# Lookup scores from stacked one-pass operands, aggregates scaled on ScalarE: one change after the attention of a fused block

## What is computed

```python
x = x + _layernorm(attention(_layernorm(x)))      # 16 heads of 16
h = _layernorm(x)
query = h @ q_proj_w.T                            # 128 wide
rq = query @ router_w.T                           # 48 wide
rk = aux_keys @ router_w.T                        # 1024 keys, 48 wide
scores = rq @ rk.T / sqrt(48) + reliability_mask
top_scores, top_idx = top_k(scores, 8)
w = softmax(top_scores)
agg = einsum('bsk,bskh->bsh', w, aux_values[top_idx])
# gate: sigmoid of the row's log variance over its mean, and of a small gelu network on h
out = h + gate[..., None] * agg
x = x + _layernorm(out)
```

## Time and profile before

| | |
|---|---|
| median of 3 runs | 3106.18 us (3104.97 to 3108.98) |
| the profiled execution | 3108.23 us, its span 3106.4 us |
| TensorE busy | 3056.3 us (98%) |
| VectorE busy | 2822.5 us (91%) |
| ScalarE busy | 2489.8 us (80%) |
| GpSimd busy | 244.1 us (8%) |
| granted TensorE clock, mean | 0.985 of 2.4 GHz |
| lookup stage, from the first `lookup_scores` | 2819 to 3106 us of the span |

### The profile page before, as it was taken

How to read it: one execution, slowest core, us unless ns; L and a number is a source line. 1 busy time by engine, 2 the same in 40 slices (tenths; PEclk the granted TensorE clock), 3 DMA queues, 4 the chain that set the end, 5 groups by cost and what they waited for, 6 DMA issues and landing times.

```text
span 3106.4 us, 67882 instructions
## 1 busy us (share of the span) xinstructions
PE 3056.3 (98%) x26937; PEld 1337.5 (43%) x26937; DVE 2822.5 (91%) x3050; ACT 2489.8 (80%) x4539; POOL 244.1 (8%) x798
## 2 busy tenths in 40 slices
PE   8999999999999999999999999999999999999997
PEld 4544443443444343444444344344444344345765
DVE  5599999999999999999999999999999999957776
ACT  6278888888888888888888888888888888864444
POOL 2400000000000000000000000000000000001012
PEclk9799999999999999999999999999999999999999
DMA  7420101010110101010202010101001010000001
GB/s 261 63 42 1 39 5 35 8 29 15 22 22 15 28 11 33 5 39 1 42 1 42 1 39 5 32 12 25 18 18 25 15 28 16 16 1 1 1 8 48
DMA packets 27400, 83.03 MB, mean 27 GB/s; under 512 B 4657, under 2 KB 15649, under 8 KB 24034
## 3 DMA queue, kind: packets, MB, share of 16 engines
q1 hardware_dynamic: 26834, 77.84, 10.8%
q0 software_dynamic: 272, 1.05, 0.1%
HBM read 57.90 MB, written 20.97 MB: 25 GB/s over the span
## 4 chain that ended last, share of the span: by engine, by line
PE 92%; DVE 4%; ACT 2%; issue 1%; DMA 0%; POOL 0%; ACTq 0%; DVEq 0%; POOLq 0%
PE ps L1152 43%; PE ps L1161 37%; PE ps L1128 3%; PE ps L1087 2%; PE ps L1171 1%; PE ps L1349 1%; PE ps L1101 1%; PE ps L1179 1%; PE ps L1079 1%; PE ps L1294 1%; DVE partial L790 1%; DVE k_raw L861 1%; DVE q_raw L854 1%; ACT k_raw L633 1%; DVE q_raw L851 1%
## 5 line engine op out<-in xcount | busy, mean ns | idle before, releaser
L790 DVE TENSOR_REDUCE partial<-ps 128x1 f32<-128x1024 f32 x2048 | 2485.9, 1224 | 130.6 <-PE ps L1128 116.2
L568 ACT ACTIVATE work<-ps 128x512 f32<-128x512 f32 x4096 | 2207.7, 597 | 361.5 <-PE ps L1152 163.7
L1128 PE MATMUL ps<-k_stack,q_stack 48*128 48x512 f32 x4096 | 1533.1, 453 | 5.5 <-DVE partial L790 5.5
L1152 PE MATMUL ps<-q_stack,k_stack 64*128 64x512 f32 x4096 | 1510.1, 448 | 0.3 <-ACT work L568 0.3
L1161 PE MATMUL ps<-work,v_head 128*32 128x256 f32 x16384 | 1296.5, 391 | 0.0
L1152 PEld LDWEIGHTS ps<-q_stack,k_stack 64*128 64x128 f32 x4096 | 632.0, 184 | 805.5 <-ACT work L568 672.1
L1128 PEld LDWEIGHTS ps<-k_stack,q_stack 48*128 48x128 f32 x4096 | 634.3, 187 | 45.9 <-DVE partial L790 40.6
L1161 PEld LDWEIGHTS ps<-work,v_head 128*32 128x32 f32 x16384 | 329.2, 108 | 698.8 <-ACT work L568 579.5
L421 POOL CAST nm_parts<-negmax 128x4 bf16<-128x4 f32 x128 | 24.8, 194 | 2275.7 <-DVE negmax L797 2275.7
L1349 PE MATMUL ps<-k_raw,q_raw 128*128 128x256 f32 x512 | 123.1, 396 | 8.3 <-DVE attn L871 8.3
L560 ACT ACTIVATE q_stack<-ps 3x512 fp32r<-3x512 f32 x128 | 75.1, 587 | 52.5 <-PE ps L1179 49.5
(11 more groups left out here) (127 smaller groups left out, 1000.5 us busy)
## 6 DMA issues: line engine op xcount, KB each, us to landing
k_stack<-qk_parts SPq DMA_DIRECT2D x96, 256.0 KB, 4.1
q_stack<-qk_parts SPq DMA_DIRECT2D x96, 256.0 KB, 4.1
qk_parts<-qk_part SPq DMA_DIRECT2D x32, 512.0 KB, 2.8
x_sb<-L_attn_x SPq DMA_DIRECT2D x8, 512.0 KB, 11.0
out<-k_raw SPq DMA_DIRECT2D x4, 512.0 KB, 3.0
out<-v_head SPq DMA_DIRECT2D x3, 512.0 KB, 2.9
k_raw<-L_ffn_aux_values SPq DMA_DIRECT2D x1, 1024.0 KB
work<-L_attn_w_qkv POOLq DMA_DIRECT2D x1, 768.0 KB, 7.5
```

What stands on the lines that cost most here:

```text
L568: act.activation(probs[:, g % DEPTH, a, :], ps[:, bank, :], ACT.Exp, scale=SCALE).then_inc(exp_done, 1)
L790: dve.tensor_reduce(partial[:, k // 4, k % 4:k % 4 + 1], ps[:, 2 * slot:2 * slot + 2, :], AX.XY, ALU.max).then_inc(max_used, 1)
L1128: last = pe.matmul(ps[:, 2 * slot + e, :], q_stack[HALF:HALF + ROWS, b1, c * CH + (k // 4) * P:c * CH + (k // 4 + 1) * P], k_stack[HALF:HA ...
L1152: pe.matmul(ps[:, bank, :], k_stack[0:HALF, b, P * g:P * (g + 1)], q_stack[0:HALF, b, at:at + CH], start=True, stop=True).then_inc(s_ready, 1)
```

## The change

- The scores are made from fp32r operands, which are rounded and go through TensorE in one pass. `ru` has the rounded rq in rows 0 to 63 and, new, what rounding left in rows 64 to 127. `rk_parts` has the rounded keys twice, one copy under the other, and their rest likewise. Two matmuls per bank give the sum of all four products. The rest of rq is made by a new VectorE step, `route_low`, once per chunk; the keys are split once, by four VectorE steps during the last attention pass.
- `gelu` reads PSUM itself, with the bias, as `ru`'s upper half is taken.
- The scaled copy of the aggregate (`keep_agg`) moves from VectorE to ScalarE, in front of each `move_wT`.
- In chunks 4 to 6 `norm_transpose` of the next chunk moves behind `aggregate(n - 1)`, and `lookup_scores(n + 3)` ahead of `transpose_picked(n + 1)`.

```diff
+        rk_parts = nc.alloc_sbuf_tensor_at("rk_parts", [P, 2, N], F32R, offset=q_at + 4 * T)
+        ru = sb("ru", [P, CH], F32R)
-        ru = work[:, 6144:6656]
...
-                act.activation(ru, ps[:, 3, :], ACT.Identity, bias=rbias).then_inc(r_ready, 1)
+                act.activation(ru[0:RUS, :], ps[0:RUS, 3, :], ACT.Identity, bias=rbias[0:RUS, :]).then_inc(r_ready, 1)
...
-                act.wait_ge(r_ready, c + 1)
-                act.activation(g1T[RUS:RUS + F1, :], ru[RUS:RUS + F1, :], ACT.Gelu).then_inc(u_ready, 1)
+                act.wait_ge(r_psum, c + 1)
+                act.activation(g1T[RUS:RUS + F1, :], ps[RUS:RUS + F1, 3, :], ACT.Gelu, bias=rbias[RUS:RUS + F1, :]
+                               ).then_inc(u_ready, 1)
...
+            def keep_agg(n):
+
+                act.wait_ge(agg_psum, n + 1)
+                act.wait_ge(wr_ready, n + 1)
+                act.activation(attn_rows[:, n, :], ps[:, 2, 0:C], ACT.Copy, scale=wrec[:, n % TPC:n % TPC + 1]
+                               ).then_inc(agg_ready, 1)
+
+            def tile_copies(n):
+
+                if n >= 2:
+                    keep_agg(n - 2)
+                move_wT(n)
...
-            move_wT(n + 3)
+            tile_copies(n + 3)
+            keep_agg(NT - 2)
             normalise(7)
+            keep_agg(NT - 1)
             normalise(8)
...
+                if n >= TPC:
+                    dve.wait_ge(agg_ready, n - TPC + 1)
                 dve.wait_ge(e_ready, n + 1)
...
-            def keep_agg(n):
-
-                dve.wait_ge(agg_psum, n + 1)
-                dve.wait_ge(wr_ready, n + 1)
-                dve.tensor_scalar(attn_rows[:, n, :], ps[:, 2, 0:C], wrec[:, n % TPC:n % TPC + 1], None,
-                                  ALU.mult).then_inc(agg_ready, 1)
+            def route_low(c):
+
+                dve.wait_ge(r_ready, c + 1)
+                dve.scalar_tensor_tensor(out=ru[RUS:P, :], in0=ps[0:RUS, 3, :], scalar=rbias[0:RUS, :],
+                                         in1=ru[0:RUS, :].bitcast(F32), op0=ALU.add, op1=ALU.subtract).then_inc(low_ready, 1)
...
+            dve.wait_ge(w3_e, 4)
+            for at in (0, RUS):
+                dve.tensor_copy(rk_parts[at:at + RUS, 0, :], rkT[0:RUS, :]).then_inc(rk_own, 1)
+            dve.wait_ge(rk_own, 2)
+            for at in (0, RUS):
+                dve.tensor_tensor(rk_parts[at:at + RUS, 1, :], rkT[0:RUS, :], rk_parts[0:RUS, 0, :].bitcast(F32),
+                                  ALU.subtract).then_inc(rk_own, 1)
             dve.tensor_copy(wcat[:, :, 0:RD], ps[:, 2, 2 * P:3 * P].rearrange("p (k n) -> p k n", k=CC)[:, :, 0:RD]
...
                 projected_stats(ahead)
+                route_low(c + 1)
                 take_top(n + 3)
...
-                pe.wait_ge(r_ready, n // TPC + 1)
+                pe.wait_ge(low_ready, n // TPC + 1)
+                if n == 0:
+                    pe.wait_ge(rk_own, 4)
...
                 for a in range(2):
-                    last = pe.matmul(sc_banks(n)[:, a, :], ru[0:RUS, P * i:P * (i + 1)],
-                                     rkT[0:RUS, CH * a:CH * (a + 1)], start=True, stop=True)
+                    for part in range(2):
+                        last = pe.matmul(sc_banks(n)[:, a, :], ru[:, P * i:P * (i + 1)],
+                                         rk_parts[:, part, CH * a:CH * (a + 1)], start=(part == 0), stop=(part == 1))
...
-                if c + 1 < NC:
                     norm_transpose(c + 1, wT_ready, n + 1)
                 if c > 0:
                     aggregate(n - 1)
+                if NC <= ahead and c + 1 < NC:
+                    norm_transpose(c + 1, wT_ready, n + 1)
+                    lookup_scores(n + 3)
...
-                lookup_scores(n + 3)
+                if ahead < NC or c + 1 == NC:
+                    lookup_scores(n + 3)
```

More of the change, by code:

```diff
@@ L234, in sandwich_kernel @@
         w3_e = sem("w3_e")
+        rk_own = sem("rk_own")
         pow_own = sem("pow_own")
@@ L247, in sandwich_kernel @@
         r_ready = sem("r_ready")
+        low_ready = sem("low_ready")
         u_ready = sem("u_ready")
@@ L667, in _ @@
                 n = c * TPC
-                move_wT(n)
+                tile_copies(n)
                 move_hT(c + 1)
@@ L673, in _ @@
                 exponentials(n + 2)
-                move_wT(n + 1)
+                tile_copies(n + 1)
                 move_ru(c + 1)
@@ L683, in _ @@
                 exponentials(n + 3)
-                move_wT(n + 2)
+                tile_copies(n + 2)
                 if c == 5:
@@ L972, in _ @@
             block_stats(3)
+            route_low(0)
             take_top(0)
@@ L980, in tile_turn @@
             def tile_turn(n):
-                if n >= 2:
-                    keep_agg(n - 2)
                 if n + 1 < NT:
@@ L1014, in _ @@
             gate_argument(0)
+            route_low(5)
             take_top(n + 3)
@@ L1028, in _ @@
             tile_turn(n + 1)
+            route_low(6)
             take_top(n + 3)
@@ L1042, in _ @@
             result(3)
+            route_low(7)
             take_top(n + 3)
@@ L1062, in _ @@
             tile_turn(n + 3)
-            keep_agg(NT - 2)
             result(7)
-            keep_agg(NT - 1)
             result(8)
@@ L1385, in _ @@
                     if c == 0:
-                        project_out(ahead, 0, 3, r_ready, 1)
+                        project_out(ahead, 0, 3, u_ready, 1)
                     else:
                         project_out(ahead, 0, 3, l_ready, c + 1)
-                if c + 1 < NC:
                     norm_transpose(c + 1, wT_ready, n + 1)
@@ L1419, in _ @@
                     lookup_scores(n + 4)
-                    learn(c + 1, 3, r_ready, c + 2)
+                    learn(c + 1, 3, low_ready, c + 2)
                 aggregate(n + 1)
```

## The result

The changed kernel takes 3111.76 us (median of 20 executions), the kernel before 3106.41 on the same chip (20 executions): ratio 1.0015, 95% interval 1.0008 to 1.0022. One of the changed kernel's 20 executions took 6323.36 us, twice the others, and is not in the ratio. The profiled execution took 3112.25, its span is 3110.5, against 3108.23 and 3106.4 before. I go by the two traces, then by the pieces.

What follows compares the result with a forecast made beforehand. A chain of 24.0 us on ScalarE and VectorE plus 9.06 on TensorE sets the chunk period. Terms -3.3 - 0.6 + 3.5 - 0.8 + 1.2 + 3.0 = +3.0 give a median of 3109.2 us, range 3102 to 3117.

Steps and rivals of the forecast that it cites:

- Start: Start to route(1): shorter scores ahead of the first transposition and at the lower clock gain 3.3 us (2.0 to 4.0).
- Three periods: route(1) to route(4): -0.5 each, -1.5 in all, or +2.7 if the clock falls; taken -0.6 us.
- Scores per tile: TensorE's scores on the chain: four fp32r passes take 0.95 us where 1.91 stood, 0.96 saved per tile.
- Copy on ScalarE: Each period: a copy of 0.45 us enters the chain just ahead of the weights' move.
- Wait for it: TensorE, once per chunk: an aggregate waits 1.9 us for ScalarE's copy, a new wait behind an exponential.
- `route_low` and the keys: VectorE's new step per chunk and the key splitting: nothing, at most 0 to 0.1 and 0.2 us.
- Chunk 4: Aggregate ahead of the transposition waits for copy(14), so hT comes late: +1.2 to +5.1 us, taken +3.5.
- Chunks 5 and 6: Chunk 5, early route: taken -0.8 us; chunk 6, hT late behind copy(22) and a normalisation: taken +1.2.
- End: copy(29) behind normalise(6), last two aggregates slide 3.3 us: +1.8, with the lower clock +3.6 to +5, taken +3.0.
- the clock falls in every new gap: Slower rival: lower clock after the waits for ScalarE's copies and before route(5), +11 us, 3117; chance 0.26.
- TensorE as the bound: Faster rival: each chunk 2.9 us shorter, seven chunks give 17 to 20, 3088 us; chance 0.14.
- the scores did become one-pass: Slower rival claimed they would not at full height and stay at 1.9 us: about +9, 3115; chance 0.06.

Runs made afterwards that it cites:

- the extra scores: The change, with the scores of one tile per chunk computed three times in chunks 0 to 3: 3108.47 us, ratio 1.0014 to the kernel before.
- the copies ahead of the exponential: The change, with most ScalarE copies ahead of the exponential and copy(29) ahead of the normalisation of piece 6: 3103.6 us, ratio 0.9994 to the kernel before.
- the scores alone: Kernel before plus one-pass scores, route_low and split keys; copies on VectorE, old TensorE order: 3102.24 us, ratio 0.998.
- scores and order: The change without its copies on ScalarE, so one-pass scores and the new TensorE order: 3101.11 us, ratio 0.9979 to the kernel before.
- the copies only: Kernel before with the scaled copies on ScalarE behind the exponential, fp32 scores and old order: 3118.51 us, ratio 1.0036.

## Why the prediction was right, and where it was not

Point by point, in the order of its sum, predicted and then measured in the traces:

- *Start*, -3.3: -3.4. The third scores, at the lower clock, took 2.06 in place of 3.78, and two more tiles gave the rest.
- *Three periods*, -0.6: -1.0. Each period without a fallen clock was 0.6 shorter, one of the new waits of 2 us cost its clock (the aggregate at 2890.33, 5.38). The -0.6 was a value taken between -1.5 and +2.7; which wait would cost its clock the argument could not say, and that so few did is in part luck. The argument held that only what stands on the chain counts. But the account was not complete. I put the period at the length of one chain; the extra scores and the copies ahead of the exponential show a second one through VectorE that ends at the same time. It is why the scores alone gave 0.77 a period, not 0.96, and why the copy's 0.45 could be taken out without gain.
- *Scores per tile*, 0.95: 1.00 to 1.10. In the run with more work for TensorE, eight more of these matmuls lengthen a group from 1.18 to 3.04, 0.23 apiece, near the 0.216 of an aggregate's instruction, which by the prediction's count streams as many columns. The Trainium skill (TensorE: Matmul & The Clock Gate, Part 3: Packing small matmuls) has a weight load overlap running matmuls only in another row group, and by that rule the prediction's estimate was 1.28 for a tile. The traces do not agree with it: 1.00 to 1.10 is less, and the loads were at least mostly hidden. `learn` behind the scores, 0.9: 0.98, and it cost nothing, as said.
- *Copy on ScalarE*, 0.45: 0.47, 0.36 of it ahead of the weights' move. *Wait for it*, 1.9: 1.86 to 2.05. *`route_low` and the keys*, nothing: the four steps for the keys took 3.9 us, and the first projected block moved by 0.09 (2771.56 to 2771.65).
- *Chunk 4*, +3.5: +3.5. hT came 6.2 us behind the exponential of tile 17 (6.0 predicted), route(5) ran at the lower clock after 4.84 us of idle (3.78), and the aggregate behind it took 4.62 where 3.62 is the warm one. The old order under the same copies takes it back, 33.33 in place of 37.34.
- *Chunks 5 and 6*, -0.8 and +1.2: -0.6 and +0.4.
- *End*, +3.0: +5.0, with +0.2 in chunk 7 before it. This is the term that was mis-sized. "The last two aggregates slide 3.3 us" held to 0.3: counted from the exponential of tile 31, copy(29) starts 3.6 later than before. The last result alone took 0.89 in place of 2.42, as said; it no longer runs beside GpSimd's addition, which is done at 3096.58. But I took the middle of a range that reached to +5, and the clock was low for nearly the whole aggregate: 6.67, while my rows of an aggregate after a wait had 5.38 and 5.72. Filling that gap with matmuls gave 3.0 back, so without the fall the end would have been +2.0, near the +1.8 of the sum before the clock.

The sum was +3.0; the traces differ by 4.0, the medians by 5.4 (4.7 by the ratio). The forecast median of 3109.2 was 2.6 too low: 1.0 in the terms, and 1.6 in the 2.05 us that I took off because the profiled execution of before stood that much above its median. The one after stood 0.5 above its own.

What the prediction did not see is the coupling. It costed copies and order as one in chunk 4 and got that right, but priced neither apart. Alone they are +10.6 and nothing. Together with them the order costs 4.7, most of it in chunk 4, where a copy behind an exponential then holds back the aggregate that now stands ahead of the transposition. With the copies ahead of the exponentials chunk 4 lost 3.0 of its 4.0. A part of the cost has no need of the copies: with them on VectorE the order costs 1.8 to 2.3 in chunk 4 as well (in scores and order route(5) also took 3.78, after 4.78 us of idle), and gets it back in chunks 5 and 6. Why it gets less back with the copies on ScalarE was not tried. Of the rivals, the one in which the clock falls in every new gap came true before route(5), before the aggregate of tile 30 and in one of the four new waits of chunks 0 to 3, and not before the aggregates of tiles 15 and 31. TensorE as the bound is refuted by the extra scores for the change and by the 0.77 of the scores alone for the kernel before, and the scores did become one-pass.

## What to carry to other kernels

An instruction moved to an engine with time to spare still pays for its place in that engine's queue: of the 11 us that the copies cost, 6.5 went by a better place in that queue, no longer behind an exponential or behind a normalisation that waited on GpSimd. Before a saving on an engine that is 98% busy is counted, put useless work on it: if the time stays, look for the other chain, and for a second one right behind it. And once a gap opens on TensorE, price it twice, as the wait and as the work behind it at the lower clock.

## What was not expected of the hardware

- Waits of equal length did not have equal effect. In the change the aggregate after 2.04 us of idle took 5.38, those after 1.86, 2.01 and 2.05 took 3.69. Over all traces the spread is wider. With the copies only, an aggregate took 5.38 after 0.94 us of idle; with the scores only, the transpositions behind 3.23 us kept the full clock:

```profile
2859.93 5.38 PE L1355 MATMUL ps<-k_raw,q_raw 128*128 128x256 f32 x16 [0.94 <-ACT attn L647]
...
2961.26 1.09 PE L1101 MATMUL ps<-ident,v_all 128*128 128x128 f32 x8 [3.23 <-ACT q_raw L645]
```

  So a gap of 1 to 3 us cannot be costed from its length alone; what else decides was not tried.
- Nor does the price follow the length of the wait. In the change an aggregate took 6.67 after 4.42 us of idle, but 6.73 after 2.08 (3049.33) and 5.93 after 4.94 (3074.84); the granted clock over them was 0.54, 0.53 and 0.60. In the kernel before the dearest was 5.72. Eight matmuls of no use ahead of the first of these brought 3.69.
- One more wait ahead of weigh on VectorE lengthens the way from an exponential's start to it from 1.15 to 1.21 us. In the change the weigh of tile 3, which has no such wait, comes after 1.15 (2848.48 to 2849.63), that of the tile after it after 1.21 (2856.16 to 2857.37). It is 0.06 per tile, on the chain, 0.2 a period: the change's 32.48 against the 32.28 of scores and order. This was read from the traces, not tried by itself.
